# Sliding-window attention in a macaron block: softmax maxima and subtractions taken for two head groups at once, and the third group's transposes placed behind the next scores

## What is computed

```python
B, S, D_IN = (2, 256, 128)
D_OUT, H, WINDOW = (128, 16, 64)
HD = D_OUT // H
qkv = jnp.einsum('bsi,oi->bso', x, w_qkv)
scores = jnp.einsum('bhqd,bhkd->bhqk', q, k) / jnp.sqrt(jnp.asarray(HD, x.dtype))
allowed = (j <= i) & (i - j < WINDOW)
scores = jnp.where(allowed[None, None], scores, jnp.asarray(-jnp.inf, x.dtype))
attn = jax.nn.softmax(scores, axis=-1)
ctx = jnp.einsum('bhqk,bhkd->bhqd', attn, v)
return jnp.einsum('bso,po->bsp', ctx, w_out) + b_out
```

## Time and profile before

| | us |
|---|---|
| median of 3 runs | 540.64 |
| lowest and highest | 540.5, 543.88 |
| the profiled execution | 541.29 |
| its span | 539.6 |

### The profile page before, as it was taken

One profiled execution on the slowest core, in us unless ns is written; L12 is line 12 of the kernel. 1 busy time (PEld: TensorE's weight loads), 2 busy tenths in 40 slices (PEclk: granted clock), 3 DMA queues, 4 the chain that ended last, 5 costly groups with the idle time before them and its releaser, 6 DMA issues.

```text
span 539.6 us, 10085 instructions
## 1 busy us (share of the span) xinstructions
PE 474.9 (88%) x3844; PEld 287.2 (53%) x3844; DVE 442.3 (82%) x892; ACT 267.8 (50%) x414; POOL 300.9 (56%) x225
## 2 busy tenths in 40 slices
PE   7998999989899989999687798789879777889996
PEld 3876767777677767677231243233323232337674
DVE  4678878878589476758978999999999999998753
ACT  2345646565555525656786546446443434330743
POOL 3348030030200012467415889999999999993581
PEclk9999999999999989999986789889989998989998
DMA  7000000000000000000009934444454354200002
GB/s 219 7 0 22 4 2 24 2 21 3 4 23 4 1 0 2 1 1 2 0 19 391 383 133 184 155 156 190 200 233 155 156 206 164 97 0 1 2 22 58
DMA packets 14402, 43.84 MB, mean 81 GB/s; under 512 B 3017, under 2 KB 10834, under 8 KB 12306
## 3 DMA queue, kind: packets, MB, share of 16 engines
q1 hardware_dynamic: 13538, 42.67, 21.0%
q10 hardware_dynamic: 816, 0.53, 0.3%
HBM read 40.78 MB, written 1.31 MB: 78 GB/s over the span
## 4 chain that ended last, share of the span: by engine, by line
PE 43%; DVE 23%; issue 15%; POOL 10%; ACT 7%; POOLq 0%; DVEq 0%; ACTq 0%
DVE hst L1078 9%; PE bk L460 6%; PE bk L466 6%; PE bk L748 5%; PE bk L1224 5%; PE bk L733 4%; POOL hC L1154 4%; PE bk L719 3%; DVE xnT L280 3%; DVE dBu L1057 3%; PE bk L705 3%; ACT bk L1313 2%; POOL powers L294 2%; ACT g L874 2%; ACT g L868 2%
## 5 line engine op out<-in xcount | busy, mean ns | idle before, releaser
L1154 POOL TENSOR_TENSOR hC<-hst,rows 128x1024 f32<-128x1024 f32 x62 | 144.3, 2349 | 13.1 <-DVE hst L1078 10.6
L1078 DVE TENSOR_TENSOR_SCAN hst<-bk,dBu 128x1024 f32<-128x1024 f32 x64 | 144.8, 2278 | 2.7 <-POOL dBu L1138 2.5
L1224 PE MATMUL bk<-hC,ident 128*128 128x512 f32 x256 | 129.5, 641 | 1.3 <-ACT ysb L1303 1.0
L1313 ACT ACTIVATE bk<-delta,aneg 128x1024 f32<-128x1024 f32 x64 | 71.5, 1118 | 97.5 <-DVE hst L1078 97.4
L1224 PEld LDWEIGHTS bk<-hC,ident 128*128 128x128 f32 x256 | 51.8, 205 | 54.5 <-issue 44.7
L287 POOL TENSOR_TENSOR veps<-mv,lneps 128x4 f32<-128x4 f32 x24 | 5.7, 238 | 124.3 <-DVE mv L259 124.2
L541 ACT ACTIVATE rows<-bk 128x512 f32<-128x512 f32 x64 | 37.7, 591 | 58.6 <-PE bk L460 58.6
L1204 PE MATMUL bk<-s,sel 96*128 96x512 bf16 x100 | 33.5, 420 | 31.4 <-DVE dBu L1057 28.5
L1057 DVE TENSOR_TENSOR dBu<-bk,du 128x1024 f32<-128x1024 f32 x50 | 60.1, 1202 | 0.8 <-PE bk L1204 0.8
L874 ACT COPY g<-bk 128x512 f32<-128x512 f32 x64 | 37.8, 590 | 23.5 <-PE bk L733 23.5
L598 DVE TENSOR_REDUCE smax<-bk 128x4 f32<-128x512 f32 x64 | 43.6, 681 | 5.9 <-PE bk L719 5.9
(11 more groups left out here) (176 smaller groups left out, 766.9 us busy)
## 6 DMA issues: line engine op xcount, KB each, us to landing
rows<-c_rows SPq DMA_DIRECT2D x16, 2048.0 KB, 7.1
rows<-c_rows SPq DMA_DIRECT2D x4, 1024.0 KB, 10.3
x<-in_x_dram SPq DMA_DIRECT2D x4, 256.0 KB, 4.8
out_dram<-x SPq DMA_DIRECT2D x4, 256.0 KB, 2.3
rows<-rows SPq DMA_DIRECT2D x4, 144.0 KB, 2.5
wmoe<-in_w_dram ACTq DMA_DIRECT2D x2, 256.0 KB, 4.9
rows<-rows SPq DMA_DIRECT2D x4, 108.0 KB, 2.3
wup<-in_upT_dram SPq DMA_DIRECT2D x1, 256.0 KB
```

Source lines behind the costliest of these rows:

```text
L1078: nc.vector.tensor_tensor_scan(hst[k % 3][:, :], dA[k % 2][:, :], dBu[k % 3][:, :], 0.0, ALU.mult, ALU.add).then_inc(m2["scan"], 1)
L1154: nc.gpsimd.tensor_tensor(hC[k % 4][:, :], hst[k % 3][:, :], crep[:, k % 12, :], ALU.mult).then_inc(m2["hC"], 1)
L1224: last = nc.tensor.matmul(bk01[:, r * CH:(r + 1) * CH], ident[:, :], hC[k % 4][:, r * CH:(r + 1) * CH], start=(k % NS == 0), stop=(k % NS ...
L1313: nc.scalar.activation(dA[k % 2][:, :], delta[:, i, :], ACT.Exp, scale=aneg[:, h * NS + n:h * NS + n + 1]).then_inc(m2["dA"], 1)
```

## The change

The eight DVE instructions of a tile's softmax become four: maxima of banks 0 and 1 in one instruction, their subtraction in one, and the same for banks 2 and 3. Each adds 2 to its semaphore, so that all waits on counts stay valid. The previous tile's context stands between the maxima and the subtraction of the second pair. Since one maximum instruction now reads banks 0 and 1 behind the semaphore of the scores, bank 1's mask is put ahead of the scores as bank 0's is. In all tiles but the last, the third group's transposes go behind the next tile's scores; in the last tile they stay behind the context transpose.

```diff
--- before.py
+++ after.py
@@ -589,19 +589,25 @@
             last.then_inc(at["qm"], 1)
 
         def attn_vector(dve):
-            def soften(t, j):
-                s3d = bank[j][:, :].rearrange("p (a k) -> p a k", a=HPG)
+            def two_banks(j):
+                return (bk01 if j == 0 else bk23)[:, :].rearrange("p (g a k) -> p g a k", g=2, a=HPG)
+
+            def maxima(t, j):
                 if j == 0:
                     dve.wait_ge(at["s"], t + 1)
                 else:
-                    dve.wait_ge(at["masked"], t * (JG - 1) + j)
-                nc.vector.tensor_reduce(smax[:, j * HPG:(j + 1) * HPG], s3d, AX.X, ALU.max).then_inc(at["max"], 1)
-                dve.wait_ge(at["max"], t * JG + j + 1)
-                m = smax[:, j * HPG:(j + 1) * HPG].rearrange("p (a o) -> p a o", o=1).to_broadcast([P, HPG, P])
+                    dve.wait_ge(at["masked"], 2 * t + 2)
+                nc.vector.tensor_reduce(smax[:, j * HPG:(j + 2) * HPG].rearrange("p (g a) -> p g a", g=2), two_banks(j),
+                                        AX.X, ALU.max).then_inc(at["max"], 2)
+
+            def subtract(t, j):
+                dve.wait_ge(at["max"], t * JG + j + 2)
+                m = smax[:, j * HPG:(j + 2) * HPG].rearrange("p (a o) -> p a o", o=1).to_broadcast([P, 2 * HPG, P])
                 if t > 0:
-                    dve.wait_ge(at["pt"], t * JG - JG + j + 1)
-                nc.vector.tensor_tensor(ssub[:, j, :].rearrange("p (a k) -> p a k", a=HPG), s3d, m,
-                                        ALU.subtract).then_inc(at["sub"], 1)
+                    dve.wait_ge(at["pt"], t * JG - JG + j + 2)
+                nc.vector.tensor_tensor(ssub[:, j:j + 2, :].rearrange("p g (a k) -> p (g a) k", a=HPG),
+                                        two_banks(j).rearrange("p g a k -> p (g a) k"), m,
+                                        ALU.subtract).then_inc(at["sub"], 2)
 
             def context(t):
                 dve.wait_ge(at["pv"], t * JG + JG)
@@ -620,12 +626,12 @@
 
             for t in range(NT):
                 c, i = t // TPC, t % TPC
-                soften(t, 0)
-                soften(t, 1)
-                soften(t, 2)
+                maxima(t, 0)
+                subtract(t, 0)
+                maxima(t, 2)
                 if t > 0:
                     context(t - 1)
-                soften(t, 3)
+                subtract(t, 2)
                 if t > 0:
                     update(t - 1)
                 if i == 0 and c + 1 < NC:
@@ -719,9 +725,8 @@
                             last = nc.tensor.matmul(bank[j][64 * s:64 * s + 64, a * P:(a + 1) * P],
                                                     qm[32 * j:32 * j + 32, a, t * P + 64 * s:t * P + 64 * s + 64],
                                                     kT[32 * j:32 * j + 32, b, r * P + 64 * s:r * P + 64 * s + P],
-                                                    start=(j > 0 and a == 0), stop=(j == 0), skip_group_check=True)
+                                                    start=(j > 1 and a == 0), stop=(j < 2), skip_group_check=True)
                 last.then_inc(at["s"], 1)
-                mask_behind(t, 1)
 
             def prob_t(t, j):
                 pe.wait_ge(at["p"], t * JG + j + 1)
@@ -779,6 +784,7 @@
 
             pe.wait_ge(set_attn, 1)
             mask_scores(0, 0)
+            mask_scores(0, 1)
             scores(0)
             mask_behind(0, 2)
             project_v(0)
@@ -792,15 +798,18 @@
                 prob_t(t, 1)
                 if t + 1 < NT:
                     mask_scores(t + 1, 0)
+                    mask_scores(t + 1, 1)
                 if t == NT - 1:
                     expert_up(0)
                 if t > 0:
                     context_t(t - 1)
-                prob_t(t, 2)
+                if t == NT - 1:
+                    prob_t(t, 2)
                 if t > 0:
                     project(t - 1)
                 if t + 1 < NT:
                     scores(t + 1)
+                    prob_t(t, 2)
                 if t == NT - 2:
                     expert_transposes()
                 if t == NT - 1:
```

## The result

| | before | after |
|---|---|---|
| median, us | 540.58 | 549.91 |
| lowest and highest (6 runs each) | 538.78, 543.88 | 547.77, 552.7 |
| the profiled execution | 541.29 | 551.28 |
| its span | 539.6 | 549.5 |

The ratio of after to before is 1.0159, 95% interval 1.0128 to 1.019: the change makes the kernel 1.6% slower. The forecast was 547.0 us, 543.0 to 550.5.

The account below looks back on a forecast made before the run. Attention was taken as bound by a PE-ACT chain, with slack on DVE. First step -0.5, three key-projection steps -0.3, eleven others +6.4, last tile +0.8: +6.4 on 540.64 gives 547.0 us, range 543.0 to 550.5.

Parts of the forecast that it names:

- the displaced transposes: Third group's four transposes on PE, moved between scores and first values: hold PE 0.53, displace a 0.32 mask, delay values +0.21 us.
- the third rival: Two-bank access on DVE is dearer: double subtraction at 1.38 us, twelve gated tiles lose 0.16 each, 548.9 us; chance 0.10.
- V to the exp: From start of PE's last values (V) through reciprocal, context and double subtraction to ACT's third exp: 2.44 us, formerly 1.74.
- Exp to scores: From ACT's third exp through context copy and PE's projection to the next scores: 1.17 us, formerly 1.50.
- DVE's room ahead of the reciprocal: Double maxima free DVE 3.5 us after the tile's first maxima start; the reciprocal comes at 4.35, so they do not delay it.
- Eleven gated steps: Scores-to-scores steps where the double subtraction holds back the third exp: +0.58 us each, +6.4 in all.
- Key-projection steps: Three tiles that also project keys; the exp stays where PE and ACT put it: -0.1 us each, -0.3 in all.
- First step: First tile, no context in DVE's way, path is DVE alone: 5.44 us becomes 4.92, counted as -0.5.
- Last tile: Third transposes keep their place but the exp is gated: +0.70 plus 0.2 from displaced transposes, of which +0.8 counted.
- Not gated: Rival: second double subtraction does not hold back the third exp, tiles cost -0.12 us, 538.6 us; chance 0.08.
- Half of it: Rival: the exp is held back, but the moved transposes fit a hole on PE; +3.3 us, 543.9 us; chance 0.14.
- DVE bounds: Rival: DVE limits the kernel, so grouping pays 16 times 0.5 us of instruction overhead, 532.6 us; chance 0.02.

Follow-up runs that it names:

- e4: Changed kernel with only the second pair split into single maxima and subtractions in the old order, first pair still merged: 541.36 us, ratio 1.0007 to the kernel before.
- e3: Changed kernel with PE's new order kept, but DVE's four single maxima and four single subtractions in their old order: 542.44 us, ratio 1.0011 to the kernel before.
- e5: Changed kernel with the context transposed on PE ahead of the masks and copied on ACT ahead of the third exp: 535.82 us, ratio 0.9901 to the kernel before.
- e1: Changed kernel with the previous tile's context moved behind the second double subtraction: 546.64 us, ratio 1.0078 to the kernel before.
- e8: Changed kernel with the previous tile's context moved ahead of the second double maxima: 576.49 us, ratio 1.0621 to the kernel before.

## Why the prediction was right, and where its sizes were off

The direction, the place and the mechanism were right: the third exp released by the double subtraction, which stands behind the wait for the last values. The size was short: 549.9 us against 547.0. Two terms of a gated step were too small, the step from projection to scores and the displaced transposes. The measured time lies 0.6 us inside the upper bound of 550.5, a bound that was set for a dearer subtraction, which did not come; that it held is in part luck. By steps:

- **Double instructions.** 1.21 and 1.22 us were taken, 1216 and 1220 ns measured. The upper bound of 1.38 was not needed, so the third rival is out. Of "510 to 533 ns" for doubling only the 510 comes from a row; doubling added 535 and 528.
- **V to the exp.** 2.44 us predicted; 133.59-131.15 = 2.44 measured.
- **Exp to scores.** 1.17 us predicted, 134.84-133.59 = 1.25 measured. The term that was mis-sized is "projection to scores is 0.32 (135.98 to 136.30)". In the tile it came from, PE's projection was not waiting, and its weight loads started 0.11 us ahead of it. Where the loads wait for ACT's copy, the step takes 0.41. Copy to projection was 0.30, not 0.32. The loads, of before and of the changed kernel:

```profile
135.87 0.30 PEld L778 LDWEIGHTS bk<-wproj,cxT 128*128 128x128 f32 x2
```

```profile
134.43 0.30 PEld L783 LDWEIGHTS bk<-wproj,cxT 128*128 128x128 f32 x2 [1.37 <-ACT cxT L889]
```

- **The displaced transposes.** +0.21 predicted; scores to last values is 131.15-126.47 = 4.68 us. Of before it is 133.06-128.15 = 4.91 in a tile with input transposes; in the changed kernel that kind has 140.02-134.84 = 5.18. So +0.27. In their new place the four transposes take 0.59 us from their start to that of the values (135.98 to 136.57), and not 0.53.
- **DVE's room ahead of the reciprocal.** The prediction read it, 4.35 us against 3.5, in a tile with input transposes. In the plain tile above, the second double maxima end at 131.74 and the reciprocal starts at 131.84: 0.10 us of room. Two other plain tiles, in which these maxima follow the subtraction 1.14 us after its start and not 1.39, leave 0.37 and 0.39 us. In one plain step (from 53.21 on), where 2.17 us of layer norm work stand ahead of the first maxima, the reciprocal (58.74) comes without any idle time behind the maxima, and that step is the one of 8.52. So there was less room for dearer double maxima than the prediction gave.
- **Eleven gated steps.** +0.58 predicted, +0.71 measured: 7.8 us where 6.4 stood. This is 1.4 of the 1.9 us by which the sum fell short.
- **Key-projection steps.** The gate does not reach them, as said, but they came out at +0.04 where -0.1 stood. It is the same 0.09 of the projection and 0.06 of the transposes.
- **First step.** -0.5 predicted, -0.31 measured. (Its 5.44 us of before are eight instructions of 0.68 to 0.69 us, not four.) A double maximum is followed by its subtraction 1.32 us after its start (127.80 to 129.12), not 1.25, and the first double maximum of a tile starts 1.32 to 1.33 us after its scores where a single one started 1.24 after them. Why these gaps are wider was not tried. They cost nothing in the gated steps, where the reciprocal still waits for PE.
- **Last tile.** +0.8 counted, +0.58 measured. The reciprocal comes 5.71 us behind the scores of before (175.91-170.20) and 5.81 now (185.59-179.78), so the displaced transposes cost 0.10 there and not 0.2. From reciprocal to projection it is 2.34 and 2.92 us, +0.58 where +0.70 stood: of before ACT's copy had itself waited 0.34 us for PE.

The sum with the measured sizes is 11 x 0.71 + 3 x 0.04 - 0.31 + 0.58 = +8.2 us, against 8.35 read from the trace's landmarks and 9.3 between the medians. The forecast had +6.4; of its miss of 2.9 us, 1.9 lie in its terms, and the rest lies outside attention.

**The rivals.** "Not gated" is refuted by ACT's 0.59 us behind the subtraction and by e4, where only that pair is split and the loss is gone. "Half of it" put the displaced transposes in a hole; in the changed kernel the last values come 0.27 us later, so they are paid in full. e3 shows them neutral only against what they leave. "DVE bounds" is out: DVE's busy time fell by 10 us and the time rose. The Trainium skill's sentence in Perfetto Trace Analysis, section Optimizing Scalar/DVE Operations, that grouping helps an engine which is saturated and that breaking up helps where bubbles arise elsewhere, agrees with e4 against the changed kernel (125.61 against 132.95 us over the fifteen steps). But e5 (120.41) shows that it is not the whole answer, since there the group stays and the order around it changes.

## What to carry to other kernels

Merging instructions publishes the first result together with the second. Before merging, read for each result when it is wanted and what stands between the two halves: here a wait for another engine stood there, and the whole pair moved behind it. Look for it in every kind of step, also in the one with the least room. Where a late result hurts only through the order of a third engine's queue, reorder that queue; an edit that is neutral alone (the moved transposes) can be what makes it pay. And take a handoff's price from a row in which the receiver was really waiting.

## What the runs showed of the hardware

- Two PSUM banks in one DVE instruction cost no more than their elements: 1216 ns against 2 x 681 for maxima, 1220 against 2 x 692 for subtractions, so 0.15 to 0.16 us is saved per instruction merged.
- Two matmuls of 128 columns followed by the scores take 0.32 us from start to start in PE's stream and 0.41 to 0.42 when their weight loads had waited for ACT's copy (changed kernel, e1, e3, e5).
- The granted clock is not the same at the same place of the program. One block of eight matmuls, with the same instructions ahead of it, took 3.68 us in five profiled executions, 5.38 in four and 5.16 in one, and in e8 two steps at 0.59 and 0.58 of the clock took 12.46 and 12.22 us instead of 9.70. What makes the one execution fall and not the other was not tried.
